# Sixteen-tile first list, the second bias on TensorE, and SyncE's address loads without bounds, in an attention block with eight experts

## The reference

```python
router_probs = softmax(x_flat @ gate_w)
expert_idx = argmax(router_probs)
for e in range(8):
    h = gelu(x_flat @ w1[e] + b1[e])
    y = h @ w2[e] + b2[e]
    out = out + where(expert_idx == e, expert_w, 0)[:, None] * y
```

## Time and profile before

| | us |
|---|---|
| runs before, median (lowest to highest) | 486.8 (486.39 to 489.99) |
| the profiled execution | 486.67 |
| its span in the trace | 484.8 |
| busy in the span: TensorE / VectorE / ScalarE / GpSimd | 365.5 / 360.3 / 324.1 / 225.1 |

### The profile page before, as it was taken

One profiled execution on the slowest core, in us unless ns is written; L12 is line 12 of the kernel. 1 busy time (PEld: TensorE's weight loads), 2 busy tenths in 40 slices (PEclk: granted clock), 3 DMA queues, 4 the chain that ended last, 5 costly groups with the idle time before them and its releaser, 6 DMA issues.

```text
span 484.8 us, 9828 instructions
## 1 busy us (share of the span) xinstructions
PE 365.5 (75%) x2851; PEld 260.2 (54%) x2851; DVE 360.3 (74%) x890; ACT 324.1 (67%) x666; POOL 225.1 (46%) x330
## 2 busy tenths in 40 slices
PE   0977367999999999998899799745012798898940
PEld 0755235666666666665566434534012697897840
DVE  5586579999999999999986333798998056465571
ACT  1348317999999999999985454857411566757730
POOL 7468316555555555555210213002556646565664
PEclk9998757999999999999987899997555899999985
DMA  9507431666766676667669993000116456656500
GB/s 208 18 7 170 124 87 52 171 166 166 170 167 157 170 182 170 169 170 166 151 132 141 149 160 116 2 0 7 40 45 191 126 147 178 178 160 182 151 25 8
DMA packets 76801, 60.36 MB, mean 125 GB/s; under 512 B 16141, under 2 KB 66321, under 8 KB 76742
## 3 DMA queue, kind: packets, MB, share of 16 engines
q1 hardware_dynamic: 71094, 55.18, 51.3%
q0 software_dynamic: 2272, 4.28, 2.6%
q10 hardware_dynamic: 3376, 0.20, 0.5%
HBM read 35.69 MB, written 24.41 MB: 124 GB/s over the span
## 4 chain that ended last, share of the span: by engine, by line
DVE 45%; PE 21%; SPq 11%; issue 11%; ACT 5%; POOL 3%; DMA 2%; DVEq 0%; POOLq 0%; ACTq 0%
DVE big L1856 13%; DVE mxs L1833 12%; DVE big L1886 5%; SPq L628 3%; SPq L613 3%; SPq L616 3%; SPq L629 3%; PE ps L1220 2%; PE ps L1647 2%; PE ps L1428 2%; PE ps L1520 2%; PE ps L1525 2%; PE ps L1631 1%; DVE u_sb L1895 1%; ACT big L979 1%
## 5 line engine op out<-in xcount | busy, mean ns | idle before, releaser
L1833 DVE TENSOR_REDUCE mxs<-ps 128x4 f32<-128x1024 f32 x64 | 73.9, 1212 | 6.8 <-PE ps L1255 6.8
L1856 DVE SCALAR_TENSOR_TENSOR big<-big,ps 128x1024 f32<-128x1024 f32 x64 | 73.9, 1214 | 3.6 <-ACT big L969 3.6
L969 ACT ACTIVATE big<-ps 128x1024 f32<-128x1024 f32 x64 | 62.4, 1028 | 9.2 <-PE ps L1393 9.0
L848 POOL DMA_INDIRECT sorted_rows<-proj,sl_i x32 | 32.1, 1002 | 51.7 <-issue 43.0
L863 POOL DMA_INDIRECT out_dram<-vb,fidx x39 | 39.4, 1009 | 26.0 <-DVE vb L2292 18.5
L1647 PE MATMUL ps<-big,xnT 128*128 x312 | 43.5, 287 | 5.3 <-ACT xnT L1180 3.9
L1255 PE MATMUL ps<-arena 96*128 96x256 bf16 x256 | 39.3, 283 | 7.8 <-issue 5.2
L1647 PEld LDWEIGHTS ps<-big,xnT 128*128 128x128 f32 x312 | 38.2, 195 | 10.1 <-issue 10.0
L769 POOL CAST mtok<-mxs 128x16 bf16<-128x16 f32 x16 | 3.2, 198 | 86.4 <-DVE mxs L1833 86.4
L1180 ACT ACTIVATE xnT<-ps,eb_sb 128x128 f32<-128x128 f32 x156 | 42.1, 377 | 0.9 <-issue 0.9
L1161 ACT ACTIVATE xnT<-vb 128x128 f32<-128x128 f32 x39 | 17.3, 491 | 36.9 <-DMA vb<-sorted_rows 36.8
(11 more groups left out here) (348 smaller groups left out, 841.3 us busy)
## 6 DMA issues: line engine op xcount, KB each, us to landing
big<-in_L_ffn_w_dram SPq DMA_DIRECT2D x39, 256.0 KB, 3.1
qk_parts<-proj SPq DMA_DIRECT2D x16, 384.0 KB, 2.9
arena<-qk_parts SPq DMA_DIRECT2D x32, 192.0 KB, 3.6
sorted_rows<-zrow SPq DMA_DIRECT2D x16, 266.0 KB, 5.7
arena<-qk_parts SPq DMA_DIRECT2D x32, 128.0 KB, 4.0
sorted_rows<-zrow SPq DMA_DIRECT2D x3, 1130.5 KB, 20.9
vb<-sorted_rows SPq DMA_DIRECT2D x39, 66.5 KB, 2.4
x_all<-in_L_attn_x_dram SPq DMA_DIRECT2D x4, 512.0 KB, 4.8
```

The lines of the kernel that those rows point to most:

```text
L969: nc.scalar.activation(W[par][:, n, :], src, ACT.Sin, scale=PI * (1 - 1e-6)).then_inc(sin_ready, 1)
L1833: nc.vector.tensor_reduce(mxs[:, b1 % 2, :, 2 * n:2 * n + 2], src, AX_X, ALU.max, negate=True).then_inc(unit_free, 1)
L1856: nc.vector.scalar_tensor_tensor(W[par][:, n, :], W[par][:, n, :], 10.0, f, ALU.add, ALU.mult).then_inc(unit_free, 1)
```

## The change

It has four parts. The second bias is cut into three bf16 parts on GpSimd in batch 4 of attention (`cut_eb2`), put into three partitions by SyncE, and added in PSUM by one matmul with a row of ones for each tile; VectorE's look-up and addition go, and statistics and finish read PSUM (`f_stats`, `f_finish`), whose bank is now free after the finish. The two `value_load` of SyncE lose their bounds. The first list is made as soon as the first half has places, ahead of the second half's variance, and the sixteen tiles behind it are read in two phases, after 12 and after 16 scattered tiles. Statistics and finish of the first two pairs are put between VectorE's last groups and the second list, their powers between GpSimd's scatters; list_out(1) follows f_down(1).

```diff
--- before.py
+++ after.py
@@ -254,9 +254,8 @@
...
-        eb2_bc = vf[:, RDEPTH * RS * ROW:RDEPTH * RS * ROW + NE * C].rearrange("p (e c) -> p e c", e=NE)
-        fres = cut_up(vf, RDEPTH * RS * ROW + NE * C, RS * C, RS, DEPTH)
-        assert RDEPTH * RS * ROW + NE * C + DEPTH * RS * C <= NT * (H * VW + 16)
+        fres = cut_up(vf, RDEPTH * RS * ROW, RS * C, RS, DEPTH)
+        assert RDEPTH * RS * ROW + DEPTH * RS * C <= NT * (H * VW + 16)
@@ -264,7 +263,8 @@
...
-        PHASES = [NK, 3 * NT // 4, NT]
+        PHASES = [3 * NK // 4, NK, 3 * NT // 4, NT]
+        FIRST = 2
@@ -272,6 +272,10 @@
...
+        eb2_parts = sb("eb2_parts", [3, NE, C], BF16)
+        ones_b = sb("ones_b", [3, P], BF16)
+        eb2_raw = late_s[0:3, 0:NE * C].rearrange("p (e c) -> p e c", e=NE)
+        eb2_high = [late_s[0:3, NE * C * (2 + i) // 2:NE * C * (3 + i) // 2].bitcast(BF16).rearrange("p (e c) -> p e c", e=NE) for i in range(2)]
@@ -590,6 +596,12 @@
...
+                if b == 2:
+                    sp.dma_start(eb2_raw.rearrange("p e c -> p (e c)"), eb2.rearrange("e c -> (e c)").partition_broadcast(3)).then_inc(eb2_in, 16)
+                if b == 5:
+                    sp.wait_ge(eb2_cut, 4)
+                    for i in range(2):
+                        sp.dma_start(eb2_parts[i:i + 1, :, :], eb2_high[i][i:i + 1, :, :]).then_inc(eb2_put, 16)
@@ -602,15 +614,14 @@
...
-            sp.dma_start(eb2_bc[:, :, :].rearrange("p e c -> p (e c)"), eb2.rearrange("e c -> (e c)").partition_broadcast(P)).then_inc(eb2_in, 16)
...
-                e = sp.value_load(exp_i[0:1, 0, k:k + 1], min_val=0, max_val=NE - 1)
+                e = sp.value_load(exp_i[0:1, 0, k:k + 1])
@@ -625,7 +636,7 @@
...
-                    blk = sp.value_load(exp_i[0:1, 1, k:k + 1], min_val=0, max_val=NBLK - 1)
+                    blk = sp.value_load(exp_i[0:1, 1, k:k + 1])
@@ -787,9 +798,20 @@
...
+            def cut_eb2():
+                pool.wait_ge(eb2_in, 16)
+                nc.gpsimd.memset(ones_b[:, :], 1.0)
+                for i in range(2):
+                    nc.gpsimd.tensor_copy(eb2_high[i], eb2_raw).then_inc(eb2_cut, 1)
+                    pool.wait_ge(eb2_cut, 2 * i + 1)
+                    nc.gpsimd.tensor_tensor(eb2_parts[:, :, :] if i else eb2_raw, eb2_raw, eb2_high[i], ALU.subtract).then_inc(eb2_cut, 1)
+                    pool.wait_ge(eb2_cut, 2 * i + 2)
...
+                if b == 4:
+                    cut_eb2()
@@ -865,12 +888,16 @@
...
-            for k in range(NL):
-                scatter(k)
-            for s in range(NP):
+            scatter(0, NK)
+            scatter(NK, NK + GT)
+            f_rstd(0)
+            scatter(NK + GT, NK + 2 * GT)
+            f_rstd(1)
+            scatter(NK + 2 * GT, NT)
+            f_store(0)
+            for s in range(2, NP):
                 f_rstd(s)
-                if s:
-                    f_store(s - 1)
+                f_store(s - 1)
             f_store(NP - 1)
 
@@ -1599,13 +1632,8 @@
...
+            list_out(0)
@@ -1642,26 +1670,28 @@
...
+                    y = ps[:, 5 + s % 3, t * C:(t + 1) * C]
+                    nc.tensor.matmul(y, ones_b[:, :], eb2_parts[:, bass.ds(e, 1), :].rearrange("p e c -> p (e c)"), start=True, stop=False)
...
-                        mm = nc.tensor.matmul(ps[:, 5 + s % 3, t * C:(t + 1) * C], fg[par][:, t, c, :], w[:, c, :],
-                                              start=(c == 0), stop=(c == EC - 1))
+                        mm = nc.tensor.matmul(y, fg[par][:, t, c, :], w[:, c, :], start=False, stop=(c == EC - 1))
...
+            pe.wait_ge(rsem["x"], 3)
...
-            list_out(0)
...
+            pe.wait_ge(eb2_put, 16 * 2)
...
-                if s == 0:
+                if s == 1:
@@ -2148,28 +2178,33 @@
...
+            def rows_made(h):
+
+                first, second = PHASES[2 * h] - TH * h, PHASES[2 * h + 1] - TH * h
+                upto = flat(4, h).rearrange("p (e t) -> p t e", t=TH)[:, first - 1:TH:second - first, :]
+                over_two = lambda v: v.unsqueeze(1).to_broadcast([P, 2, NE])
+                chain(nc.vector.tensor_tensor(made[:, 2 * h:2 * h + 2, :], upto, over_two(row_from[:, :]), ALU.subtract))
+                chain(nc.vector.tensor_tensor(made[:, 2 * h:2 * h + 2, :], made[:, 2 * h:2 * h + 2, :], over_two(side[:, :]), ALU.mult))
...
+                rows_made(0)
+                chain(nc.vector.tensor_scalar(full[:, 1:3, :], made[:, 0:2, :], -(TS - 1) / 2.0, 1.0 / TS, ALU.add, ALU.mult))
+                whole_blocks(0, 2)
+                list_of(2)
...
+                rows_made(1)
+                nc.vector.tensor_scalar(full[:, 3, :], made[:, 2, :], -(TS - 1) / 2.0, 1.0 / TS, ALU.add, ALU.mult)
+                chain(nc.vector.tensor_scalar(full[:, 4, :], made[:, 3, :], (TS - 1) / 2.0, 1.0 / TS, ALU.add, ALU.mult))
+                whole_blocks(2, 4)
@@ -2224,9 +2259,11 @@
...
+            first_list()
...
+            list_taken(0)
@@ -2242,61 +2279,57 @@
...
-            first_list()
...
-            list_taken(0)
-            for g in range(GH, NG - 1):
-                add_shift(g)
-                add_x(g)
+            def f_stats(s):
+                par, j, n = s % 2, s % DEPTH, len(tiles_of(s))
+                if s >= DEPTH:
+                    dve.wait_ge(f_out[j], 16 * RS * (s // DEPTH))
+                dve.wait_ge(fs["y_ps"], s + 1)
+                for t in tiles_of(s):
+                    st = nc.vector.bn_stats(fst[:, par, t, 0:6], ps[:, 5 + s % 3, t * C:(t + 1) * C])
+                st.then_inc(dve_own, 1)
+                nc.vector.tensor_scalar(fidx_f[:, j, 0:n], frow[s % RDEPTH][:, 0:n, C + 1], 0.0, 2.0 * NT * P, ALU.is_equal, ALU.mult).then_inc(dve_own, 1)
+                own_steps[0] += 2
+                dve.wait_ge(dve_own, own_steps[0] - 1)
+                for t in tiles_of(s):
+                    ag = nc.vector.bn_aggr(fst[:, par, t, 6:8], fst[:, par, t, 0:6])
+                dve.wait_ge(dve_own, own_steps[0])
+                nc.vector.scalar_tensor_tensor(fidx[:, j, 0:n], fidx_f[:, j, 0:n], -1.0, frow[s % RDEPTH][:, 0:n, C + 1], ALU.add, ALU.add).then_inc(fs["idx"], 1)
+                chain(ag)
+                nc.vector.scalar_tensor_tensor(fst[:, par, 0:n, 8], frow[s % RDEPTH][:, 0:n, C], LN_EPS, fst[:, par, 0:n, 7], ALU.max, ALU.add).then_inc(fs["var"], 1)
+
+            def f_finish(s):
+                par, j = s % 2, s % DEPTH
+                dve.wait_ge(fs["r"], s + 1)
+                for t in tiles_of(s):
+                    nr = nc.vector.tensor_scalar(fz[par][:, t, :], ps[:, 5 + s % 3, t * C:(t + 1) * C], fst[:, par, t, 6:7], fst[:, par, t, 9:10],
+                                                 ALU.subtract, ALU.mult)
+                nr.then_inc(fs["z"], 1)
+                dve.wait_ge(fs["z"], s + 1)
+                for t in tiles_of(s):
+                    add = nc.vector.scalar_tensor_tensor(fres[j][:, t, :], frow[s % RDEPTH][:, t, 0:C], frow[s % RDEPTH][:, t, C + 3:C + 4], fz[par][:, t, :],
+                                                         ALU.add, ALU.add)
+                add.then_inc(fs["res"], 1)
+
+            add_shift(GH)
+            add_x(GH)
+            add_shift(GH + 1)
+            add_x(GH + 1)
+            f_stats(0)
+            add_shift(GH + 2)
+            add_x(GH + 2)
+            f_finish(0)
+            f_stats(1)
             second_list()
             add_shift(NG - 1)
             add_x(NG - 1)
...
-            def f_weigh(s):
-                par, j, n = s % 2, s % DEPTH, len(tiles_of(s))
-                if s >= 2:
-                    dve.wait_ge(fs["res"], s - 1)
-                dve.wait_ge(fs["y_ps"], s + 1)
-                for t in tiles_of(s):
-                    k = RS * s + t
-                    e = dve.value_load(exp_i[0:1, 0, k:k + 1], min_val=0, max_val=NE - 1)
-                    z = nc.vector.tensor_tensor(fz[par][:, t:t + 1, :], ps[:, 5 + s % 3, t * C:(t + 1) * C].unsqueeze(1), eb2_bc[:, bass.ds(e, 1), :], ALU.add)
-                z.then_inc(fs["z"], 1)
-
-                if s >= DEPTH:
-                    dve.wait_ge(f_out[j], 16 * RS * (s // DEPTH))
-                nc.vector.tensor_scalar(fidx_f[:, j, 0:n], frow[s % RDEPTH][:, 0:n, C + 1], 0.0, 2.0 * NT * P, ALU.is_equal, ALU.mult).then_inc(dve_own, 1)
-                dve.wait_ge(fs["z"], s + 1)
-                for t in tiles_of(s):
-                    st = nc.vector.bn_stats(fst[:, par, t, 0:6], fz[par][:, t, :])
-                st.then_inc(dve_own, 1)
-                own_steps[0] += 2
-                dve.wait_ge(dve_own, own_steps[0] - 1)
-                nc.vector.scalar_tensor_tensor(fidx[:, j, 0:n], fidx_f[:, j, 0:n], -1.0, frow[s % RDEPTH][:, 0:n, C + 1], ALU.add, ALU.add).then_inc(fs["idx"], 1)
-                dve.wait_ge(dve_own, own_steps[0])
-                for t in tiles_of(s):
-                    ag = nc.vector.bn_aggr(fst[:, par, t, 6:8], fst[:, par, t, 0:6])
-                chain(ag)
```

(60 more changed lines are left out.)

10 lines of the change are left out of this document (3 added, 7 removed).

## The result

The changed kernel takes 493.46 us (median of eight runs, 491.83 to 498.26), the kernel before 487.77 beside it (eight runs, 486.38 to 489.99). The ratio is 1.0128, with a 95% interval of 1.0099 to 1.0157: slower by 5.7 us, where 480.0 was forecast, with 473.5 to 488 as its range. The profiled execution took 493.23 us, its span 491.4.

The account below looks back on a forecast made before the run. VectorE was taken to bound attention, SyncE's issuing much of the expert stage, GpSimd the end. Expert-stage saving of 11.4 us less 4.7 for the attention stall gave -6.7 from 486.67: 480.0 us, range 473.5 to 488.

Parts of the forecast that it names:

- the stall: Attention, batch 4 onward: GpSimd's cut delays the split of u and later loads, costing 4.7 us, bounds 0 and 7.
- The bias matmul, 0.10 us a tile: TensorE, expert stage: one bf16 bias matmul per tile costs 0.10 us, making a pair 4.0 us, with 4.36 as other end.
- The second list "no earlier": VectorE, between the lists: second list taken at 387.2 us before the stall, against 386.06 before, so no gain there.
- 1 us for the clock: TensorE, third pair's down-projection: idle time before it may lower the clock, so 1 us is added to 393.5.
- SyncE: Expert row loads: without bounds an issue takes 0.84 us instead of 1.11, 3.4 a pair, and SyncE is no longer the bound.
- The first rows: Start of the expert stage: first row load near 365.6 us, which is 360.9 plus the stall, instead of 367.72.
- The cut: GpSimd, attention batch 4: cutting the bias takes 7.1 us, as three partitions cost as much as 128; VectorE loses 3.7, then 1.0.
- the rival that hid the cut: Attention: GpSimd is quick on three partitions, so no stall and 475.3 us; chance 0.20.
- GpSimd: Expert stage: GpSimd needs 3.25 to 3.89 us a pair, a little less than TensorE's 4.0; 9.1 us remain behind TensorE's end.
- the pace stays: Expert pairs: address work eats the saving, or TensorE with bias at 4.36 replaces SyncE; 486.2 us, chance 0.14.
- The interleaving: Between the lists: pair 0 not down-projected before 385 holds back scatters, stores and second list by 10 us; 490.0, chance 0.11.
- signs of being wrong: Profile after: hole missing, pairs taking much more than 4.0 us, or first down-projection not ending some 5 us earlier.

Follow-up runs that it names:

- order run: Changed kernel with VectorE making the second list before the first pair's statistics, TensorE transposing it after the second f_up, GpSimd's scatters before the first roots: 483.27 us.

## Why the prediction was wrong

The time was 13.5 us above the forecast, and TensorE's end 13.6: with the stall the forecast had it at 458.2 + 4.7 = 462.9, and it was 476.5. Two steps make it up.

- **The bias matmul, 0.10 us a tile: mis-sized, and the step that failed.** It took 0.355, above even the upper end of 0.287. (That end was misread: the 312 records of the earlier trace rows are two for each of 156 products, so 0.287 is the mean length of one record, and no price of a matmul.) From the end of f_down(2) to TensorE's end the forecast had 63.7 us (399.2 to 462.9) and the trace has 72.5 (404.0 to 476.5): 8.8 us. The price was taken from a matmul near in type and length, but that one has 128 rows next to matmuls of 96, and not 3 among 128. With 128 rows the bias costs 0.11, so the 0.10 was right for the form that the row had, and the form was what mattered. With that alone mended the time is 486.06, 2.7 us below before; the forecast had 6.7. The trace before may hold a nearer row: in attention the weight loads of 32-row matmuls (L1393) and those of the 128-row ones behind them (L1226) each follow 0.21 us of idle time marked "issue" (at 132.05 and 132.88 us). The mark stands at other places too, so it is a hint and no price.
- **The second list "no earlier", and 1 us for the clock: 4.8 us short.** f_down(2) ended at 404.0 instead of 399.2. The list was taken 2.8 us after the forecast's 391.9 (387.2 and the stall), because pair 0 ended at 382.5, also 2.8 after the forecast's 379.7, and the list stood behind its statistics. Pair 0 was late by a term without a row: from the start of its up-projection to its end the forecast has 8.6 us (366.4 to 375), where the kernel before took 11.8 (373.28 to 385.08) and the kernel after 11.8 (370.68 to 382.51). The rest is in the main the clock, granted at 0.57 and 0.75 in the two windows from 390 us: the third pair's products took 2.08 us a tile instead of 1.16. The order run shows that the step also missed the point: VectorE stood idle for 10.8 us ahead of the list's place, and the list needs nothing from pair 0.

Pair 0's last products in the kernel before, then its first and last ones in the kernel after:

```profile
383.01 2.07 PE L1647 MATMUL ps<-big,xnT 128*128 x8 [0.15 <-ACT xnT L1180]
...
370.68 3.74 PE L1659 MATMUL ps<-xnT,big 128*128 128x128 f32 x16 [0.46 <-ACT xnT L1195]
...
380.73 1.78 PE L1677 MATMUL ps<-big,xnT 128*128 x8
```

What held:

- **SyncE**: 0.82 to 0.86 us an issue (0.84 forecast), and off the chain.
- **The first rows** at 365.26 (365.6 forecast), the start of pair 0's up-projection at 370.68 (371.1).
- **The cut**: casts of 1.03 us, subtractions of 2.15 and 2.13 (1.03 and 2.26 forecast); 6.7 us in all (7.1); holes of 2.83 and 1.47 (3.7 and 1.0), whose sum came nearer than its parts, 4.3 for 4.7; 5.3 by the run that moves it, with some 2 us of uncertainty. Three partitions cost as much as a full tile's length says, so the rival that hid the cut fell.
- **GpSimd** was no bound, and the tail behind TensorE 8.8 us (9.1).

Of the rivals, *the pace stays* came true by its second cause: TensorE with the bias took SyncE's place, at 4.50 us a pair where 4.36 was the most. *The interleaving* came true only in small part: it asked for pair 0 at 381.7 or later without the stall, 386.4 with it, and pair 0 ended at 382.5. That the two delays could add was not considered. Of the signs of being wrong two showed: pairs took 4.50, and the first down-projection ended 2.6 us earlier than before, not 5.

## What to carry to other kernels

A row of the trace prices an operation only for the form that it has: for a short matmul among long ones look at the number of contraction rows first, and pad a bias of a few rows with zero rows until it has the form of its neighbours. A step that one engine makes for all the others (here a list) belongs ahead of whatever waits for those others; an idle time of 10 us ahead of it in the trace is the sign. When a change bundles parts, each wants its own price: here one part alone was worth 10 us, and three with small flaws took 16 back.

## What the runs showed of the hardware that was not expected

- A one-pass 16-bit matmul of 3 or 64 rows between matmuls of 128 rows costs 0.355 us in steps from start to start, one of 96 or 128 rows 0.11. The duration of its own record, 0.22 to 0.23 us, is the same in all four.
- An fp32 matmul of one row is two records and costs 0.61 us a tile among fp32 matmuls of 128 rows.
- The check of a register load's bounds on SyncE is worth 0.25 to 0.29 us for each issue (1.11 to 0.82 to 0.86), and 10.2 us of this kernel.
